# Two small stages of a two-layer block rewritten: first queries by token rows, second output projection in three passes

## What is computed

```python
# layer 0, queries: 16 heads of 16 columns, normalised per head
q = _ln((x @ Wq + bq).reshape(b, s1, H, HD), qn_w, qn_b)   # (t - mean) * rsqrt(var + 1e-6) * w + b
# the keys get a norm with weight kn_w too; scores are q . k / 4
# layer 1, output projection: 16 heads of 128 columns
out = out.reshape(B, Sq, H * D)      # (16, 56, 2048)
return out @ Wo                      # (2048, 256)
```

## Time and profile before

| | us |
|---|---|
| median of the runs | 2333.1 |
| profiled execution | 2329.33 |
| its span | 2327.6 |
| from the first queries' first VectorE operation to the keys' first product | 17.53 to 65.79 |
| from projection 1's first product to the copy of its second sums | 2195.74 to 2245.80 |

### The profile page before, as it was taken

One profiled execution on the slowest core, in us unless ns is written; L12 is line 12 of the kernel. 1 busy time (PEld: TensorE's weight loads), 2 busy tenths in 40 slices (PEclk: granted clock), 3 DMA queues, 4 the chain that ended last, 5 costly groups with the idle time before them and its releaser, 6 DMA issues. The chain is left out here.

```text
span 2327.6 us, 46500 instructions
## 1 busy us (share of the span) xinstructions
PE 2092.5 (90%) x16696; PEld 1690.0 (73%) x16696; DVE 1704.9 (73%) x2327; ACT 1230.5 (53%) x2243; POOL 1233.7 (53%) x995
## 2 busy tenths in 40 slices
PE   4899999999999569999999786778999999999875
PEld 2688788788788347777777633557999999999643
DVE  5788888888888566666666333758899999999366
ACT  1688888888888315555555212574444444444302
POOL 1566666666666223443343032353898988989200
PEclk8999999999999769999999868899999999999987
DMA  3524323323332412343332053484223323221400
GB/s 91 157 95 161 120 98 147 118 112 138 117 124 112 164 51 94 142 145 118 116 116 86 16 205 92 117 206 159 107 86 110 119 80 111 84 106 43 176 11 16
DMA packets 115908, 259.92 MB, mean 112 GB/s; under 512 B 48001, under 2 KB 85538, under 8 KB 106642
## 3 DMA queue, kind: packets, MB, share of 16 engines
q1 hardware_dynamic: 111938, 246.79, 30.4%
q10 hardware_dynamic: 2304, 7.34, 0.8%
q0 software_dynamic: 1536, 3.94, 0.5%
HBM read 153.71 MB, written 108.28 MB: 113 GB/s over the span
## 5 line engine op out<-in xcount | busy, mean ns | idle before, releaser
L350 DVE TENSOR_REDUCE rk<-n_sq 128x1024 f32 (+2 forms) x384 | 466.0, 1214 | 120.9 <-ACT n_sq L298 117.5
L298 ACT ACTIVATE n_sq<-n_slot 128x1024 f32<-128x1024 f32 (+1 forms) x384 | 394.2, 1027 | 141.1 <-PE n_slot L258 131.7
L256 PE MATMUL n_slot<-n_wh,n_yh 128*128 128x512 f32 (+1 forms) x768 | 317.8, 414 | 9.5 <-PEq L444 9.5
L1665 ACT ACTIVATE a_pr<-a_sc 128x448 f32<-128x448 f32 (+1 forms) x384 | 204.9, 544 | 191.3 <-PE a_sc L1596 178.9
L1729 DVE TENSOR_REDUCE a_mpart<-a_pre 112x2 f32<-112x1024 f32 (+1 forms) x192 | 218.8, 1184 | 118.3 <-PE a_pre L1567 118.3
L258 PE MATMUL n_slot<-n_wh,n_yl 128*128 128x512 f32 (+1 forms) x768 | 303.3, 395 | 0.0
L257 PE MATMUL n_slot<-n_wl,n_yh 128*128 128x512 f32 (+1 forms) x768 | 302.0, 393 | 0.0
L1368 POOL TENSOR_TENSOR p_S<-p_S,a_mb 128x896 f32<-128x896 f32 x94 | 255.2, 2751 | 69.3 <-ACT a_mb L1413 69.3
L1368 POOL TENSOR_TENSOR a_S<-a_S,a_mb 128x896 f32<-128x896 f32 (+1 forms) x89 | 240.7, 2740 | 39.2 <-ACT a_mb L1413 39.2
L230 POOL TENSOR_TENSOR n_khat<-n_kb,n_rs 128x240 f32<-128x240 f32 x192 | 114.3, 595 | 233.8 <-DVE n_rs L365 233.7
L1426 ACT ACTIVATE p_S<-p_S 128x896 f32<-128x896 f32 x96 | 91.5, 953 | 161.7 <-POOL p_S L1368 158.4
(11 more groups left out here) (361 smaller groups left out, 4665.7 us busy)
## 6 DMA issues: line engine op xcount, KB each, us to landing
vdram<-n_v SPq DMA_DIRECT2D x16, 1632.0 KB, 5.3
a_v<-vdram SPq DMA_DIRECT2D x16, 1632.0 KB, 6.9
kTdram<-n_kT SPq DMA_DIRECT2D x16, 1484.0 KB, 5.0
a_kT<-kTdram SPq DMA_DIRECT2D x16, 1484.0 KB, 7.5
n_yT<-in_ctxT SPq DMA_DIRECT2D x16, 750.0 KB, 8.6
yhdram<-n_yh SPq DMA_DIRECT2D x16, 750.0 KB, 6.4
yldram<-n_yl SPq DMA_DIRECT2D x16, 750.0 KB, 8.6
a_yh<-yhdram SPq DMA_DIRECT2D x16, 750.0 KB, 4.2
```

Source lines behind the costliest of these rows:

```text
L256: pe.matmul(dst, high, wh[:, cols], start=True, stop=False)
L298: act.activation(sq[0:n, w, :], slot[w][0:n, :], ACT.Square).then_inc(slot_free, 1)
L350: dve.tensor_reduce(g.rk[0:n, b, j, 8 * s:8 * s + 8], sq[0:n, (2 * j + s) % 3, :].rearrange("p (h d) -> p h d", h=8), X, ALU.add)\
L1665: act.activation(pr[0:n, s % 4, unit, :], sc[(2 * s + unit) % 3][0:n, 0:HALF], ACT.Exp).then_inc(p_ready, 1)
```

## The change

**First queries.** Tokens now lie on the partitions, 112 a tile, in four groups of two tiles. The query weights and the bias are centred per head in place (`centre_queries`, on VectorE inside the layer norm block), so that no centring product is needed; the bias enters as a product of a row of ones with the bias row. Per group: ScalarE squares, VectorE sums by head (112x32), ScalarE takes the root, VectorE inverts the 112x32 and multiplies three times over 112x512 (norm, gain, subtraction of each head's last column), TensorE turns both results to feature rows, ScalarE and VectorE write the high and the low part. The loads are issued in the layer norm block, the constants of later stages behind them. GpSimd has nothing; ScalarE and VectorE split the first context. The stores of the queries move to the head of SP's stream in the keys block, and are waited for at that block's end.

**Projection 1.** Both operands are split: `Mh`, `Ml` from M, `oh`, `ol` from the attention outputs, in a ring of four units. A unit `u` is one head of one half of the batches: six F32R products of 128x448. ScalarE makes all high parts, GpSimd `Ml`, VectorE `ol` of units 0 to 15 and of 22, 24, ..., 30, GpSimd that of the others. The second load is in two pieces, four batches each, so units from 16 on have two operations of 224 columns for each part.

```diff
 def load_splits(sp, g):
+    sp.dma_start(g.wqa[:, :, :], g.a["L0_Wq"]).then_inc(g.wqa_in, 16)
+    sp.dma_start(g.qrow[:, :, :], g.a["qrow"]).then_inc(g.wqa_in, 16)
+    sp.dma_start(g.cols[:, 0:6], g.a["cols0"]).then_inc(g.wqa_in, 16)
     sp.dma_start(g.yT[0][:, :], g.a["ctxT"][0]).then_inc(g.yT_in[0], 16)
+    sp.dma_start(g.ones[:, :], g.a["ones"]).then_inc(g.ones_in, 16)
+    sp.dma_start(g.wall[:, :], g.a["L1_Wk"]).then_inc(g.w1_in, 16)
     sp.dma_start(g.wkv[:, 0:D], g.a["L0_Wk"]).then_inc(g.w0_in, 16)
     sp.dma_start(g.wkv[:, D:2 * D], g.a["L0_Wv"]).then_inc(g.w0_in, 16)
     sp.dma_start(g.kbias[:, :], g.a["bk0"]).then_inc(g.w0_in, 16)
-    sp.dma_start(g.wall[:, :], g.a["L1_Wk"]).then_inc(g.w1_in, 16)
     sp.dma_start(g.yT[1][:, :], g.a["ctxT"][1]).then_inc(g.yT_in[1], 16)
...
+    for dst, src in ((g.blk, "blk"), (g.hmask, "hmask"), (g.bkdrow, "bkd")):
+        sp.dma_start(dst[tuple(slice(None) for _ in dst.shape)], g.a[src]).then_inc(g.consts_in, 16)
+    for dst, src in zip(g.router, ("gw", "gb", "eid", "trash", "low", "pair")):
+        sp.dma_start(dst[tuple(slice(None) for _ in dst.shape)], g.a[src]).then_inc(g.router_in, 16)
...
+def centre_queries(dve, g):
+    by_head = lambda t: t.rearrange("p (h d) -> p h d", d=HD0)
+    parts = ((g.wqa[:, :, :].rearrange("p k n -> p (k n)"), 0, 2 * H), (g.qrow[:, 0, :], 2 * H, 3 * H))
+    dve.wait_ge(g.wqa_in, 48)
+    for t, lo, hi in parts:
+        dve.tensor_reduce(g.qmean[:, lo:hi], by_head(t), X, ALU.add).then_inc(g.wqa_steps, 1)
+    for n, (t, lo, hi) in enumerate(parts):
+        dve.wait_ge(g.wqa_steps, 1 + n)
+        dve.scalar_tensor_tensor(out=by_head(t), in0=g.qmean[:, lo:hi].unsqueeze(2).broadcast_to([P, hi - lo, HD0]),
+                                 scalar=-1.0 / HD0, in1=by_head(t), op0=ALU.mult, op1=ALU.add).then_inc(g.wqa_steps, 1)
...
+def high_context(act, g):
+    act.wait_ge(g.yT_in[0], 16)
+    act.activation(g.yh[0][:, :], g.yT[0][:, :], ACT.Copy).then_inc(g.y_high, 1)
+
+
+def low_context(dve, g):
+    dve.wait_ge(g.y_high, 1)
+    dve.tensor_tensor(g.yl[0][:, :], g.yT[0][:, :], g.yh[0][:, :], ALU.subtract).then_inc(g.y_split, 1)
...
+            for half in range(2):
+                for n in range(2):
+                    sp.dma_start(g.qcdram[:, :, 2 * half + n, :].rearrange("b p q -> p b q"),
+                                 g.q4[:, half, n, :].bitcast(F32).rearrange("p (b q) -> p b q", b=B)).then_inc(g.qc_stored, 16)
             sp.dma_start(g.xbuf[0:E * CAP, :], g.a["empty"]).then_inc(g.empty_out, 16)
             sp.dma_start(g.ypairs[0:2 * T, :], g.a["zeros"]).then_inc(g.empty_out, 16)
```

```diff
+            for s in range(G0):
+                for a in range(GT):
+                    t, dst = GT * s + a, ps[s][0:TT, a * D:(a + 1) * D]
                     for k in range(2):
-                        mm = pe.matmul(ps[half][:, n, 0:HALF], wqa[:, k, half * P:(half + 1) * P],
-                                       g.xnT[:, k, n * HALF:(n + 1) * HALF], start=(k == 0), stop=(k == 1))
+                        pe.matmul(dst, g.xnT[:, k, t * TT:(t + 1) * TT], g.wqa[:, k, :], start=(k == 0), stop=False)
+                    mm = pe.matmul(dst, g.ones[0:1, 0:TT], g.qrow[0:1, 0, :], start=False, stop=True)
...
+            def turn(s, src, dst, done):
+                for k in range(2):
+                    for a in range(GT):
+                        mm = pe.transpose(dst[:, k * GW + a * TT:k * GW + (a + 1) * TT],
+                                          src[:, GT * s + a, k * P:(k + 1) * P], g.ident[0:TT, 0:TT])
+                mm.then_inc(done, 1)
+            for s in range(G0):
+                pe.wait_ge(normed, s + 1)
+                turn(s, z, ps[s], n_psum)
+                pe.wait_ge(d_ready, s + 1)
+                turn(s, zd, tp[s], d_psum)
...
+            high_context(act, g)
             high_weights(act, g)
             act.wait_ge(eps_set, 1)
...
+            square(0)
+            root(0)
+            square(1)
+            root(1)
+            square(2)
+            high_part(0)
+            square(3)
+            root(2)
+            root(3)
+            small(0)
+            high_part(1)
+            small(1)
+            high_part(2)
+            small(2)
+            high_part(3)
+            small(3)
```

```diff
+            col = lambda which: g.cols[:, which]
+            for out, one, other in ((BOTH_LAST, SHIFT_LAST, KEY_LAST), (BOTH, SHIFT, KEY)):
+                dve.scalar_tensor_tensor(out=col(out), in0=col(one), scalar=HD0 ** -0.5, in1=col(other),
+                                         op0=ALU.mult, op1=ALU.mult).then_inc(weighed, 1)
+            dve.scalar_tensor_tensor(out=prod[:, 0, :], in0=g.qrow[:, 1, :], scalar=HD0 ** -0.5, in1=g.qrow[:, 2, :],
+                                     op0=ALU.mult, op1=ALU.mult).then_inc(weighed, 1)
+            dve.wait_ge(weighed, 3)
+            dve.tensor_tensor(col(BOTH), col(BOTH), col(BOTH_LAST), ALU.subtract).then_inc(weighed, 1)
             split_first_weights(dve, g)
...
+            low_context(dve, g)
+            low_weights(dve, g)
...
+            def normalise(s):
+                dve.wait_ge(rooted, s + 1)
+                dve.reciprocal(ss[:, s, :], ss[:, s, :]).then_inc(inverted, 1)
+                dve.wait_ge(inverted, s + 1)
+                dve.tensor_tensor(by_head(of(z, s)), ps[s][0:TT, :].rearrange("p (h d) -> p h d", d=HD0),
+                                  ss[:, s, :].unsqueeze(2).broadcast_to([TT, GT * H, HD0]), ALU.mult).then_inc(normed, 1)
+                dve.wait_ge(normed, s + 1)
+                dve.tensor_tensor(of(zs, s), of(z, s), prod[0:TT, :, :].broadcast_to([TT, GT, D]), ALU.mult).then_inc(scaled, 1)
+                dve.wait_ge(scaled, s + 1)
+                heads = by_head(of(zs, s))
+                dve.tensor_tensor(by_head(of(zd, s)), heads, heads[:, :, HD0 - 1:HD0].broadcast_to([TT, GT * H, HD0]),
+                                  ALU.subtract).then_inc(d_ready, 1)
+
+            def low_part(s):
+                dve.wait_ge(high, s + 1)
+                dve.scalar_tensor_tensor(out=q4(s, 1), in0=turned(tp[s]), scalar=col(BOTH), in1=q4(s, 0),
+                                         op0=ALU.add, op1=ALU.subtract).then_inc(split, 1)
+            sums(0)
+            normalise(0)
+            sums(1)
+            normalise(1)
+            low_part(0)
+            sums(2)
+            sums(3)
+            normalise(2)
+            low_part(1)
+            normalise(3)
+            low_part(2)
+            low_part(3)
```

```diff
+    NB, M, UNITS, WABS = B // 2, g.M, 2 * H, H + 6
+    by_pool = lambda u: H <= u < WABS or u >= WABS and u % 2 == 1
+    parts = lambda u: 1 if u < H else 2
+    pool_lows = lambda u: sum(parts(v) for v in range(u + 1) if by_pool(v))
+    highs = lambda u: sum(parts(v) for v in range(u + 1))
+    dve_lows = lambda u: highs(u) - pool_lows(u)
...
+            for at, o in ot[1]:
+                sp.dma_start(o, g.odram[NB + at:NB + at + o.shape[1]].rearrange("b c n -> c b n")).then_inc(ot_in[1], 16)
...
+            for u in range(UNITS):
+                half, h = u // H, u % H
                 if half == 0:
+                    pe.wait_ge(M_low, h + 1)
+                if by_pool(u):
+                    pe.wait_ge(pool_low, pool_lows(u))
+                else:
+                    pe.wait_ge(dve_low, dve_lows(u))
+                for dk in range(2):
+                    dst, cols = ps[4 + 2 * half + dk][:, 0:HALF], slice(dk * P, (dk + 1) * P)
+                    high, low = [t[u % 4].rearrange("p b q -> p (b q)") for t in (oh, ol)]
+                    pe.matmul(dst, Mh[:, h, cols], high, start=(h == 0), stop=False)
+                    pe.matmul(dst, Mh[:, h, cols], low, start=False, stop=False)
+                    mm = pe.matmul(dst, Ml[h][:, cols], high, start=False, stop=(h == H - 1))
+                mm.then_inc(used, 1)
+                if u == WABS:
                     pe.wait_ge(g.wabs_sums, 3)
                     pe.matmul(ps[0][:, 0:3], g.ones[:, :], g.wabs[:, :], start=True, stop=True).then_inc(g.wsum_psum, 1)
...
+        def _(act):
+            for u in range(UNITS):
+                if u % H == 0:
+                    act.wait_ge(ot_in[u // H], 16 * len(ot[u // H]))
+                if u < H:
+                    act.activation(Mh[:, u, :], M[:, u, :], ACT.Copy).then_inc(M_high, 1)
+                if u >= 4:
+                    act.wait_ge(used, u - 3)
+                for high, o in pieces(u, oh):
+                    act.activation(high, o, ACT.Copy).then_inc(o_high, 1)
...
+            for h in range(H):
+                pool.wait_ge(M_high, h + 1)
+                pool.tensor_tensor(Ml[h], M[:, h, :], Mh[:, h, :], ALU.subtract).then_inc(M_low, 1)
+            for u in range(UNITS):
+                if by_pool(u):
+                    pool.wait_ge(o_high, highs(u))
+                    for high, low, o in pieces(u, oh, ol):
```

(84 more changed lines are left out.)

157 lines of the change are left out of this document (51 added, 106 removed).

## The result

The changed kernel takes 2315.3 us in the median of four runs (2314.2 to 2316.3), beside 2333.0 for the kernel before: a ratio of 0.9922, with an interval of 0.991 to 0.9935. That is 17.7 us less, where 29.0 were forecast, and 1.3 us outside the range. The profiled execution has a span of 2312.2 us in place of 2327.6.

The account below looks back on a forecast made before the run. It took loads, VectorE and the store to bound the first queries and TensorE projection 1; 23.5 + 5.5 = 29.0 us less, taken from the median 2333.1, gave 2304 us, range 2297 to 2314.

Parts of the forecast that it names:

- so the 24 of 256 columns take 10.4: First queries: TensorE's 24 products of 256 columns take 10.4 us at full clock, 20.8 at 1.2 GHz.
- Near 30 all four groups are in PSUM, two VectorE groups ahead of need: First queries: TensorE finishes all four groups' products near 30 us, before VectorE needs them.
- the sum: Whole kernel: 23.5 us from the first queries plus 5.5 from projection 1, 29.0 us less.
- Its bound: First queries at the lower clock throughout: last group at 38.3, its chain ends near 44.5, a gain of 21 us.
- The rest of the queries: First queries: VectorE's stream to 25.0, four groups of 3.55 us, waits 2.5, first key product at 42.2, 23.5 us less.
- The second rival: Keys' beginning: first batches wait for the moved stores, at most 11.3 us come back, total 2315.4; chance 0.05.
- The moved stores: Keys: the queries' four stores at the head of SP's stream were costed at nothing.
- the lower clock cost 1.5 us as charged: Projection 1: TensorE loses about 1.5 us to the lower clock level after its idle time, as before.
- a wait of 0.7: Projection 1: unit 26's low pieces, behind a rounding, done at 2231.9 where TensorE wants them at 2231.2.
- Unit 30, just in time in the sum: Projection 1: unit 30's low parts arrive just in time, so no wait was charged there.
- The first rival: Projection 1 from unit 22: VectorE's and GpSimd's work takes turns, gain there only 0.9 us, total 2308.7; chance 0.20.
- The third rival: TensorE stays at 1.2 GHz in projection 1 as well as the queries: slower, 2342 us; chance 0.05.

Follow-up runs that it names:

- the new order: Kernel with 128-row bias and third rounding in the last stage, plus VectorE's low parts of units 26, 28, 30 between single rounding operations: 2296.6 us, 0.985 of before.

## Why the prediction was wrong

**The step that failed** is in the first queries: "so the 24 of 256 columns take 10.4", and "Near 30 all four groups are in PSUM, two VectorE groups ahead of need". It took full clock for granted. The kernel before shows 1.00 at this place, but its first eight products of 448 columns took 8.14 us there, where 0.76 each would be 6.1, so even before the engine wasn't at full pace from the first product on. With one-row bias products among them the 24 took 23.3 us. With 128 rows, nothing else changed, they took 13.1, the groups were in PSUM at 30.4, and the total gain was 29.9 us, where the sum said 29.0. That this total fits so well is in part luck: the two places give 23.3 + 3.9 = 27.2 us, the keys take 2.0 of it back, and the rest lies in stages that nobody changed, such as 1418.5 us between the keys and projection 1 in this profile where it was 1421.4 before.

**Its bound failed too.** "At the lower clock throughout, the last group is there at 38.3" and a gain of 21: a tile of one-row and other products takes 3.10 us there, where three products of 128 rows take 2.56, so the last came at 41.0. And behind the last product I put one group's chain. In fact two groups' work stood there, since VectorE's low part of group 0 heads its queue and waits for transposes behind all products; that order was in the diff, and I had counted the queue only for the case in which TensorE is early. The kernel with the low parts last puts 5.2 us on it.

**The rest of the queries was right.** VectorE's first reduction came at 24.7 (25.0 forecast), with 128 rows the first two groups stood 3.5 us apart (3.55), VectorE's waits were 0.39, 0.39, 0.62 and 1.17, 2.6 us (2.5), and the keys' first product at 42.47 (42.2). The reciprocals took 0.35, not 0.2. The second rival named 2315.4 us, and 2315.3 were measured: that is chance. The moved stores cost nothing at the keys' beginning, since the first reduction there leads by the same 11.9 us as the first product. The 1.6 us that the keys lose later were in no term of the sum.

**Projection 1** was right in its mechanism and off by 1.6 us: 46.2 where 44.6 were forecast. A unit took 1.22 us (1.23) and its first product came 1.9 us behind the block's start (1.7); the lower clock cost 1.5 us as charged, eight steps of 0.37 in place of 0.20 until 2190.3. The term that was mis-sized is "a wait of 0.7": it was 2.5 us, in two pieces. The sum had a whole rounding ahead of unit 26's two low pieces, at 3.2 and 0.75 us. Beside GpSimd's pieces they took 3.56 and 1.61 (2217.32 to 2220.88, and from there to 2222.49), 1.2 us more, which is what unit 26's wait of 1.93 has over 0.7. Unit 30, just in time in the sum, waited 0.59; its own two pieces took 1.62. At the end VectorE's third rounding held the copies back by 0.5, as the sum had it.

**The first rival** was right that both are stretched, and wrong that this alone sets the end. With the stretching still there (1.49 us for an operation of the roundings), the new order brought the copies 2.3 us earlier; with GpSimd's pieces given to VectorE they came only 0.4 us earlier. Two pieces of each, side by side, stand 0.77 us apart on both engines; alone they stand 0.30 apart on VectorE and 0.63 on GpSimd, so strictly in turn a pair would take 0.93. The Trainium skill (SBUF — State Buffer, section "SBUF: two separate sides") has the exclusive lock, held for the whole instruction, under which it would be that sum; these rows show less. Which parts of the two overlap, no run shows. **The third rival**, that the clock stays at 1.2 GHz, came true where I had charged only 2.5 us for it, in the queries, and not in projection 1, where its products run at full pace from 2190.3 on.

## What to carry to other kernels

A product of one row takes TensorE no less time than one of 128 (1.12 us here at the lower clock, beside 0.85) and can keep the clock down for all its neighbours: bring a bias by 128 rows, if the row stands on all partitions. When a forecast rests on an engine that is "ahead of need", work it out once at the lower clock with the other engines' queues as written, not with one chain behind the last product. And where a long side job shares an engine with short feeds, put the feeds between its operations.

## What the runs showed of the hardware

TensorE can be busy in every microsecond of a stretch (8.00 of 8.00 from 33 to 41) and yet be granted 0.50. The Trainium skill (TensorE: Matmul & The Clock Gate, "Part 1: The HAM clock gate") ties the level to how busy the engine has been. In these runs the profile's busy share is the same at both levels: 8.00 of 8.00 at 0.50 here, 7.90 of 7.90 at 1.00 with 128 rows. What differs is eight products of the 24. With one row the clock stayed down through all of them; with none, or with 128 rows in their place, TensorE came to full pace after the first two to four tiles.

The granted clock's column isn't all: in the kernel with 128 rows the first two tiles ran at half the pace of the others (2.56 and 1.30 us) while the column shows 1.00 for both. The distance of equal products is the safer reading. All four kernels with one-row products began the block at full pace and fell to 0.50 between 19.2 and 19.6 us; all eight others with the new queries began at half pace and came up between 21.0 and 23.8. Where this difference at the first product comes from, no run shows. So the fall itself can't be put down to the one-row products; that the clock didn't come back can.

GpSimd also stretches a VectorE operation on one input: the rounding's 1.03 us became 1.38 beside GpSimd's subtraction, and that took 1.44 in place of 0.67, though it met a low part of VectorE as well. With the low parts between the roundings, a GpSimd piece that met only two operations of the roundings took 1.45, and the first of these 1.49. Not every operation on one input does this: beside VectorE's sums of the ternary weights (1.88 us, as in the kernel before) GpSimd's pieces took 0.67.
